# A selective scan followed by attention: output tiles of 32 times by four batches, one iteration behind the scan

## The reference, cut

```python
xr, gate = jnp.split(x @ W_in.T, 2, axis=-1)          # 1024 + 1024 channels
xn = layernorm(silu(conv4(xr + t_emb))) * ln_g + ln_b
Bm, Cm, dt = jnp.split(xn @ W_xproj.T, 3, axis=-1)    # 16 states each
def step(h, inputs):
    ad, bd, xt, ct = inputs
    h = jnp.clip(h * ad[:, :, None] + bd[:, :, None] * xt[:, None, :], -10.0, 10.0)
    yt = jnp.einsum('bd,bdh->bh', ct, h)
    return (h, yt)
_, ys = jax.lax.scan(step, h0, ...)                   # 1024 times
y = ys.transpose(1, 0, 2) + D * xn
x = x + y * silu(gate) @ W_out.T
...
x = x * s1[:, None, :]
x = (x - mu) * rsqrt(var + 1e-5)                      # per time, over 512
q, k, v = x @ q_weight, ...
```

## Time and profile before

| what | before |
|---|---|
| median of 3 runs | 2919.54 us (2915.05 to 2922.15) |
| the profiled execution's own time | 2919.2 us |
| its span | 2917.4 us |
| mean granted clock of PE | 0.965 |
| PE busy | 2700.9 us (93%) |
| DVE busy | 2012.0 us (69%) |
| POOL busy | 1258.6 us (43%) |
| ACT busy | 1191.2 us (41%) |
| bytes moved by transfers | 423.97 MB, 145 GB/s |

### The profile page before, as it was taken

The page is one execution under the profiler, slowest core; times in us unless marked ns, Lnnn a source line. Parts: engine busy times, 40 slices in busy tenths (PEclk is TensorE's granted clock), DMA queues, the critical chain, the costliest instruction groups (busy, mean ns, idle before and its releaser), DMA issues. The chain is left out here.

```text
span 2917.4 us, 54601 instructions
## 1 busy us (share of the span) xinstructions
PE 2700.9 (93%) x20561; PEld 1470.9 (50%) x20562; DVE 2012.0 (69%) x2121; ACT 1191.2 (41%) x2041; POOL 1258.6 (43%) x572
## 2 busy tenths in 40 slices
PE   7999955999999999999879999969999999999999
PEld 3444323666666666666558777833333333333337
DVE  2788866998888888888653333357777777777626
ACT  3677851211222211212231222126666666666641
POOL 0000001346555464555441221016667777777763
PEclk9999967999999999999889999979999999999999
DMA  3246474677777777777634334372334344354246
GB/s 105 93 159 208 177 249 99 144 165 165 170 164 170 167 169 162 173 162 168 177 124 155 136 148 169 130 201 68 81 88 124 92 123 115 88 127 119 83 170 228
DMA packets 255677, 423.97 MB, mean 145 GB/s; under 512 B 54760, under 2 KB 122984, under 8 KB 249144
## 3 DMA queue, kind: packets, MB, share of 16 engines
q1 hardware_dynamic: 172952, 332.71, 40.0%
q10 hardware_dynamic: 82592, 89.57, 13.0%
HBM read 260.91 MB, written 163.08 MB: 145 GB/s over the span
## 5 line engine op out<-in xcount | busy, mean ns | idle before, releaser
L909 DVE CUSTOM_DVE_ANT_0 b_h<-b_h,b_bx,b_bounds_all 128x512 f32<-128x512 f32 x1024 | 825.7, 806 | 148.8 <-PE b_bx L1043 98.8
L1609 DVE TENSOR_REDUCE e_half_max<-ef_banks 128x4 f32<-128x2048 f32 x256 | 586.3, 2294 | 235.1 <-PE ef_banks L1562 235.1
L1752 POOL TENSOR_TENSOR e_pair_sum<-e_probs 128x2048 f32<-128x2048 f32 x128 | 586.7, 4584 | 265.9 <-PE ef_banks L1601 214.4
L1721 ACT ACTIVATE e_probs<-ef_banks 128x512 f32<-128x512 f32 x1024 | 556.0, 595 | 311.5 <-PE ef_banks L1576 311.5
L1576 PE MATMUL ef_banks<-e_qs,e_ks 97*128 97x512 f32 x1024 | 383.1, 453 | 3.9 <-DVE e_half_max L1609 3.6
L1094 ACT COPY b_y_stage<-b_y_psum 128x128 f32<-128x128 f32 x256 | 68.6, 268 | 652.5 <-PE b_y_psum L1053 651.2
L1576 PEld LDWEIGHTS ef_banks<-e_qs,e_ks 97*128 97x128 f32 x1024 | 155.0, 189 | 332.1 <-ACT e_probs L1721 311.9
L1025 POOL TENSOR_TENSOR b_b_weights<-b_bd,b_mask_b 128x512 fp32r<-128x512 f32 x64 | 82.6, 1290 | 552.7 <-POOLq L836 459.2
L1043 PE MATMUL b_bx<-b_x_moving,b_b_weights 24*128 24x512 f32 x1024 | 256.3, 496 | 54.6 <-POOL b_c_weights L1027 27.4
L1053 PE MATMUL b_y_psum<-b_h,b_c_weights 128*32 128x128 f32 x8224 | 278.5, 276 | 0.5 <-ACT b_y_stage L1094 0.5
L1586 PE MATMUL ef_banks<-e_probs,e_v 128*32 128x512 f32 x2048 | 274.5, 608 | 0.5 <-ACT e_probs L1721 0.4
(11 more groups left out here) (225 smaller groups left out, 4076.4 us busy)
## 6 DMA issues: line engine op xcount, KB each, us to landing
b_x_moving<-xn_parts SPq DMA_DIRECT2D x252, 128.0 KB
e_ks<-qk_parts ACTq DMA_DIRECT2D x42, 512.0 KB, 4.8
e_qs<-qk_parts ACTq DMA_DIRECT2D x84, 256.0 KB, 3.5
xn_full<-a_xn SPq DMA_DIRECT2D x32, 512.0 KB, 3.2
xn_parts<-a_hi SPq DMA_DIRECT2D x64, 256.0 KB, 2.5
xn_parts<-a_lo SPq DMA_DIRECT2D x64, 256.0 KB, 2.5
silu_gate<-b_sg ACTq DMA_DIRECT2D x64, 256.0 KB, 7.1
scan_out<-b_y_stage ACTq DMA_DIRECT2D x256, 64.0 KB, 3.8
```

Source lines behind the costliest of these rows:

```text
L909: return nc.vector._custom_dve(bass.dve_ops.TENSOR_ADD_SAT, **operands)
L1609: nc.vector.tensor_reduce(out=half_max[:, u // UNITS % 2, :, r // NH, r % NH], in_=(banks[:, u % 2 * GROUP:(u % 2 + 1) * GROUP] if u < FIR ...
L1721: nc.scalar.activation(probs[:, g % 4, h, :], p_exp[h % 2], ACT.Exp).then_inc(exps, 1)
L1752: nc.gpsimd.tensor_tensor(out=pair_sum[:, t % 2], in0=probs[:, (2 * t) % 4], in1=probs[:, (2 * t + 1) % 4], op=ALU.add).then_inc(paired, 1)
```

## The change

Everything in it turns on the shape of an output tile. It now is 32 times of all four batches, so the tile of one scan iteration can be worked on one iteration later (`LAG` = 1).

- `load_mixed`, `load_y`, `load_x` and `load_x1` address DRAM as 4 batches × 32 times. xn and gate are loaded behind the second half's moving rows, no longer behind the first's.
- `load_moving` waits for `read` two pairs sooner; `load_bd` comes behind it and one half ahead.
- `take_turned` of half 0 of the next tile stands ahead of the iteration's last readout copy and its stores.
- W_out is loaded at the scan's start and split in iterations 0 and 1; the spread of B is issued in the block before. Output tiles start in iteration 1.
- The drain does the products of tile 30 and tile 31 in full. Seven x1 tiles are prepared there (five normalisations inside the projection's first steps); the eighth is loaded at its end and scaled (now by DVE), measured and normalised in steps 4 and 5 of batch 0. Batch 0's body is written out apart from the loop.
- `y_stage` and `sg` use the storage of `pj.v_rows`. In the last iteration two of four stores are issued by SP. The input array `x_tiles` is laid out in the new order of rows.

```diff
     def load_x1(self, sp, n, q):
-        sp.dma_start(self.x1[:, q, :], self.X1.rearrange("(q b) t c -> b q t c", b=BATCH)[bass.ds(n, 1)].rearrange("o q t c -> (o q) t c")[q]).then_inc(self.x_in[q], 16)
...
+        sp.dma_start(self.x1[:, q, :], self.X1.rearrange("(q i) (b t) c -> b q i t c", q=NQ, b=BATCH)[bass.ds(n, 1)].rearrange("o q i t c -> (o q) i t c")[q]).then_inc(self.x_in[q], 16)
...
 
-    LAG = P // STEPS
+    LAG = 1
     OUT_LAG = LAG + 1
...
-        y_stage = sb("y_stage", [128, 2, T // 4, 128], f32)
+        pj.late_rows()
+        y_stage, sg = (pj.v_rows[:, 2 * i:2 * i + 2, :] for i in range(2)); y_stage = y_stage.rearrange("p i (q c) -> p i q c", c=128)
...
+                spread_b(sp, Bx, spread, SEQ // PHASES * STATES, range(PHASES))
...
+        def load_mixed(sp, j):
             sp.wait_ge(gated, START + j)
-            sp.dma_start(xn, Xn[b, bass.ds(tq * P, P), :]).then_inc(xn_in, 16)
+            sp.dma_start(xn, Xn[:, bass.ds(j * STEPS, STEPS), :]).then_inc(xn_in, 16)
             for half in range(2):
                 sp.wait_ge(sg_out[half], START + j * 16 + 16)
             sp.dma_start(sg_in, SG[bass.ds(j, 1)].rearrange("o p c -> (o p) c")).then_inc(xn_in, 16)
-        def load_y(sp, j, tq, b, it):
+        def load_y(sp, j):
             for i in range(2):
-                sp.wait_ge(y_out[i], START + it * 64)
-            sp.dma_start(y[:], Y[bass.ds(tq * P, P)].rearrange("t (h b) c -> b t h c", h=2)[b]).then_inc(y_in, 16)
-        def load_x(sp, j, tq, b):
+                sp.wait_ge(y_out[i], START + j * 64 + 64)
+            sp.dma_start(y[:], Y[bass.ds(j * STEPS, STEPS)].rearrange("t (h b) c -> b t h c", h=2)).then_inc(y_in, 16)
+        def load_x(sp, j):
             sp.wait_ge(x1_ready, START + j)
-            sp.dma_start(x[:], I["x"][b, bass.ds(tq * P, P), :]).then_inc(res_in, 16)
+            sp.dma_start(x[:], I["x"][:, bass.ds(j * STEPS, STEPS), :]).then_inc(res_in, 16)
...
-        def sp_loop(sp, it, j, tq=None, b=None, store=False, before=None, more=True):
+        def sp_loop(sp, it, store=True, x=True, more=True, load_d=False):
+            j = it + (-1)
             for i in range(2):
-                sp.wait_ge(read, START + it * PAIRS + (10 + 8 * i))
-                load_bd(sp, it, i)
+                sp.wait_ge(read, START + it * PAIRS + (8 + 8 * i))
                 load_moving(sp, it, i)
                 if i == 0:
-                    if j is not None:
-                        load_mixed(sp, j, tq, b)
+                    sp.wait_ge(w_ready[1], START + it * 2 + (-1))
+                    load_bd(sp, it, 1)
+                elif more:
+                    sp.wait_ge(w_ready[0], START + it * 2 + 1)
+                    load_bd(sp, it + 1, 0)
             if more:
                 load_tile(sp, it + 1)
-            if j is not None:
-                load_y(sp, j, tq, b, it)
-                if store:
-                    store_x1(sp, j + (-2))
-                if before is not None:
-                    load_x(sp, j + (-1), *before)
...
+            if load_d:
+                sp.wait_ge(out_split, START + 4)
+                sp.dma_start(d_row, I["D"].rearrange("(o n) -> o n", o=1).to_broadcast([P, INNER])).then_inc(d_in, 16)
+            load_mixed(sp, j)
+            load_y(sp, j)
+            if store:
+                store_x1(sp, j + (-2))
+            if x:
+                load_x(sp, j + (-1))
+
+
+        def pool_loop(pool, it, j, out=False, split=True, low=False, split_out=False):
             for i in range(2):
                 if i == 1 and split:
                     split_low(pool, it)
+                if i == 1 and split_out:
+                    for c in range(4):
...
-        def act_loop(act, it, j, more=True, split_out=False):
+        def send_y(e, it, i, parts):
+            dst = Y[bass.ds(it * STEPS + i * T, T)].rearrange("(q s) r (j c) -> j (s r) q c", s=4, j=4)
+            for part in parts:
+                e.dma_start(dst[part], y_stage[32 * part:32 * part + 32, i]).then_inc(y_out[i], 16)
+
+        def act_loop(act, it, j, more=True, split_out=False, ahead=None):
             for q in range(STEPS // 4):
                 i = (4 * q) // T
-                if q == 0 and j is not None:
-                    take_turned(act, j, 0)
                 if q == 1 and j is not None:
                     take_turned(act, j, 1)
                 if q == 7 and j is not None:
                     take_out(act, j)
+                if q == 7 and ahead is not None:
+                    take_turned(act, ahead, 0)
                 act.wait_ge(read, START + it * PAIRS + (BEFORE + 2 * q + 4))
                 if (4 * q) % T == 0:
                     act.wait_ge(y_out[i], START + it * 64)
                 nc.scalar.copy(y_stage[:, i, q % (T // 4), :], y_psum[:, 0:128]).then_inc(y_free, 1)
                 if (4 * q + 4) % T == 0:
                     act.wait_ge(y_free, START + it * (STEPS // 4) + (q + 2))
-                    dst = Y[bass.ds(it * STEPS + i * T, T)].rearrange("(q s) r (j c) -> j (s r) q c", s=4, j=4)
-                    for part in range(4):
-                        act.dma_start(dst[part], y_stage[32 * part:32 * part + 32, i]).then_inc(y_out[i], 16)
+                    send_y(act, it, i, range(4) if more or i == 0 else range(2))
 
                 if q == 0:
                     take_gate(act, it, 0)
...
             def _(sp):
+                sp.dma_start(w_out_plain, I["w_out_t"].rearrange("(m p) n -> p m n", p=P)).then_inc(out_in, 16)
                 load_tile(sp, 1)
-                spread_b(sp, Bx, spread, SEQ // PHASES * STATES, range(PHASES))
...
-                sp.dma_start(w_out_plain, I["w_out_t"].rearrange("(m p) n -> p m n", p=P)).then_inc(out_in, 16)
...
+                sp.wait_ge(w_ready[0], START + 1)
+                load_bd(sp, 1, 0)
+                sp_loop(sp, 1, False, False, load_d=True)
+                sp_loop(sp, 2, False)
+                with sp.Fori(3, LOOPS - 1) as it:
+                    sp_loop(sp, it)
+                sp_loop(sp, LOOPS - 1, more=False)
+                sp.wait_ge(y_free, START + LOOPS * (STEPS // 4) + 1)
+                send_y(sp, LOOPS - 1, 1, range(2, 4))
...
+                pool_loop(pool, 1, 0, split_out=True)
+                pool_loop(pool, 2, 1, low=True)
...
+                load_mixed(sp, last)
+                sp.wait_ge(x1_out, START + (last - 3) * 16)
+                for q in early_tiles[:3]:
+                    pj.load_x1(sp, 0, q)
+                load_y(sp, last)
+                store_x1(sp, last - 2)
+                load_x(sp, last - 1)
+                for q in early_tiles[3:]:
+                    pj.load_x1(sp, 0, q)
+                sp.dma_start(pj.w_u[:], I["u_t"].rearrange("(k p) n -> p k n", p=P)).then_inc(pj.u_in, 16)
+                store_x1(sp, last - 1)
+                load_x(sp, last)
+                for i in range(2):
+                    sp.wait_ge(sg_out[i], START + LOOPS * 16)
+                    sp.wait_ge(y_out[i], START + LOOPS * 64)
                 pj.spread_rows(sp)
-                store_x1(sp, last - 1)
-                load_x(sp, last, NQ - 1, BATCH - 1)
                 store_x1(sp, last)
+                sp.wait_ge(x1_out, START + TILES * 16)
+                pj.load_x1(sp, 0, NQ - 1)
...
+                for g in range(2):
+                    take_turned(act, last - 1, g)
+                pj.split_high(act, 0)
+                take_out(act, last - 1)
+                for g in range(2):
+                    take_turned(act, last, g)
+                for n in (1, 2):
+                    pj.split_high(act, n)
+                pj.root(act, 0, slice(0, NQ - 1))
+                for q in range(2):
                     pj.normalise(act, 0, q)
                 take_out(act, last)
...
+                add_x(dve, nc.vector, last - 2)
+                mix(dve, nc.vector, last)
+                pj.split_low(dve, 0)
+                pj.stats_of(dve, 0, early_tiles[:3])
+                add_x(dve, nc.vector, last - 1)
+                pj.split_low(dve, 1)
+                pj.split_low(dve, 2)
+                pj.stats_of(dve, 0, early_tiles[3:])
+                pj.add_eps(dve, 0, slice(0, NQ - 1))
+                pj.invert_std(dve, 0, slice(0, NQ - 1))
                 add_x(dve, nc.vector, last)
...
-            with e.Fori(0, BATCH - 1) as b:
+            body(0, True, True)
+            with e.Fori(1, BATCH - 1) as b:
                 body(b, True)
             body(BATCH - 1, False)
...
                                 nc.vector.tensor_tensor(out=lo[:, e % 2, :], in0=p_qk[e % 2][:], in1=hi[:, e % 2, :].bitcast(f32), op=ALU.subtract).then_inc(lo_ready, 1)
+                        if first and s == 4:
+                            pj.scale_x1(dve, nc.vector, 0, NQ - 1, True)
+                            pj.stats_of(dve, 0, (NQ - 1,))
+                            pj.add_eps(dve, 0, slice(NQ - 1, NQ))
+                        if first and s == 5:
```

(4 more changed lines are left out.)

192 lines of the change are left out of this document (65 added, 127 removed).

## The result

The changed kernel takes 3119.12 us (median of four runs, 3109.13 to 3122.01) against 2920.02: 1.068 times as long, 95% interval 1.065 to 1.071. The forecast was 2938, with a range that ended at 3010. The profiled execution's span is 3120.0 us, PE's mean clock 0.929.

The account below looks back on a forecast made before the run. The scan was taken as DVE's chain, with PE busy 28.8 us per iteration and able to catch up little. Scan +44.5, ahead of it 0, drain -26 and projection +0.5 gave +19 on 2919.2: 2938 us, range 2858 to 3010.

Parts of the forecast that it names:

- Which engines the loads run on: Scan: the loads of xn, y and x, with 4 in front of their sources, run on 4 of 16 engines.
- How long an iteration gets: Scan: 31.5 us per iteration, bounds 29.0 and 33.5; from iteration 1's start 974.5 against 930.0 us, +44.5.
- the sum over one of the four engines: Scan, from an iteration's start S: transfer times on one engine added up; y lands at S + 21.7, moving rows S + 28.8.
- 24 GB/s per engine for y, x and the moving rows behind them: Scan loads: rate taken from the spread of B; xn and y 5.5 us each, x 2.7.
- y's place: SP's second burst in the scan: y directly behind xn and gate, with 1.5 us put in for ACT's stores.
- The idle quarter: DMA engines in the scan: about a quarter idle between bursts, which slower transfers can use up before costing anything.
- A queue behind the queue: Rival, chance 0.15: in the scan late y delays mix, turn, stores and next y; 34.5 us an iteration, 3025 us.
- All 16 engines: Rival, chance 0.11: SBUF's 128 partitions spread the scan's loads; 29.0 us an iteration, drain -39, 2852 us.
- Enough idle time: Rival, chance 0.22: same four engines, late transfers fall into the scan's idle quarter; 29.8 us an iteration, 2888 us.
- Ahead of the scan: Before iteration 1: the earlier spread of B and the w_out load together change 0 us, between -11 and +8.
- The drain: Scan's end to the projection's first transpose: two output tiles left instead of five, 77.2 to 51 us; -26, between -39 and -20.
- The turned tile ahead of the copy: Scan: with earlier moving rows returns at most 1.3 us per iteration of PE's waits; 29.0 us at best.

Follow-up runs that it names:

- turn_after_stores: The changed kernel with the first take_turned back at the next iteration's head, behind the readout copy and the stores: 3120.0 us against 3119.1.
- time_major: The changed kernel with output tile rows ordered time, batch, so that the sources of xn, y and x begin with 32: 2833.6 us, 2835.5 when repeated.

## Why the prediction was wrong

**Which engines the loads run on: right.** 3.8 of 16 engines were busy in xn's window, and a loss of this size appears and disappears with the first dimension of the source. The Trainium skill (DMA: Bandwidth & Descriptors, "Why a DMA increments its semaphore by 16 and not by 1") has the rule of the prediction, the largest number up to 16 that divides the slowest dimensions of both sides, and the trace agrees with it: 4 in front, 3.8 engines. The same section of the Trainium skill says that a transfer takes the lowest-numbered engines, so that the eight-row transfers of moving rows would share the four. The trace has no engine's number, but its packets fit: 32 of the 96 rows came late. That is 4 engines with one row each of all eight transfers; if the eight-row transfers lay elsewhere, it would be 16.

**How long an iteration gets: wrong, 31.5 us against 37.4.** Scan +44.5 forecast, +219.4 measured; this is nearly the whole error. The step that failed is the sum over one of the four engines, above all its rate, and with it the overlap that was to hide what was late. The short iterations have the forecast length, 31.6 us, but not by the sum's terms: xn is issued up to 6.4 us before S, where the sum had it run from S + 7.3, so that agreement is partly luck. The long ones, 43.1 us, the sum did not foresee.

1. *24 GB/s per engine for y, x and the moving rows behind them.* I took the rate of the spread, which ran alone. xn does run at 26 once the moving rows are through. But y and x overlap the next moving rows, and then the mean of the 16 engines was 9.2 GB/s. The packets' own times in the trace say the same of the loads: on SP's queue a packet of 2 KB took 93 ns on average from 1122 to 1124, and 370 ns from 1126 to 1128. This is no effect of the narrow loads. In the kernel before, with moving rows beside xn on 16 engines, stands

```profile
1006.00:1008.00 2.00, 2.00 (x20) 1.29 (x12) 1.89 (x4) 0.27 (x1) 0.40 (x1) 1.00 0.97 141
```

which is 9.1 GB/s per engine. A milder warning stood in a row that I used for something else: 181 GB/s at 0.76 in the earlier trace rows is 14.9. So y took 13.6 us from issue to use in the iteration shown (1120.58 to 1134.16, POOL's row, not shown) where the sum had 7.5, and the moving rows 22.0 us from issue to PE's release where it had 12.3: S + 39.0 in place of S + 28.8, and S + 43.8 in the usual long one. Even x alone, 2.7 us in the sum, cost 117 us in all.

2. *y's place.* The sum let y start right behind the gate, at S + 14.2, and counted 1.5 us for ACT's stores, not that y waits for them. In the iteration shown this did no harm: y was issued at S + 14.1. In the usual long one it was issued at S + 17.3, and the next moving rows behind it at S + 20.1 in place of S + 16.5. That the stores land late because a quarter of each stands behind xn is my reading; no run isolates it.
3. *The idle quarter.* I let it absorb what was late. It is a mean of 16 engines. xn at 1114 and the rest of y and x at 1134 do run in it, but on some 4 engines while the others have little or nothing to do, and a third of the next moving rows needs just these four.

On top of these comes PE's clock, which the sum left out. In the earlier trace rows PE has 1.00 over the scan; here it is 0.90, since every long iteration has a stretch at 0.50 at its stall, and PE's busy time per iteration grew from 28.8 to 32 × 476.18 / 514 = 29.6 us.

**The rivals.** "A queue behind the queue", to which I gave 0.15, named the right thing, late loads that make later ones late, and held ACT's wait for the turn to be a link. turn_after_stores shows that this link is real but small, 1.7 us an iteration, and paid back by what PE gains. Its 34.5 us an iteration was too low as well. "All 16 engines" gave 2852; with xn, y and x on 16 engines the kernel takes 2834 to 2867. For "Enough idle time" I let the sum turn negative below 30.4 us an iteration; by its own terms that is 31.5 - 19 / 29 = 30.8.

**Ahead of the scan:** 0 forecast, +3.4 measured. **The drain:** -26 forecast, -19.0 measured, outside its bound of -20. The sum had y at +24, the last addition at +46 and the first transpose at +51 behind the scan's end; they came at +27.4, +49.1 and +58.2. The addition waited for ACT's copy (2.05 us) and not for x. SP's issue, 5.50, 4.88 and 10.61 us, was not in the sum; how much of the delay is its doing is not shown. With xn, y and x on 16 engines it is -38.5, the bound of -39. **The projection:** +0.5 forecast, -1.2 measured: the moved work is hidden. **The turned tile ahead of the copy:** with the moving rows I allowed 1.3 us an iteration and took PE's 28.8 us of busy time as a floor, "29.0 at best". Alone it returns 35 us in the kernel before and 41 in time_major, and time_major's iteration takes 28.4 us with PE busy throughout: the 28.8 still held time that could go.

## What to carry to other kernels

Before a tile's rows are regrouped, look at what the first dimension of each transfer's source becomes: here 4 in front of 32 in place of 128 cost 252 to 285 us, and with 32 in front of 4 the kernel is faster than before. Take an engine's rate from rows in which it does what it will do then, with the same neighbours; GB/s divided by 16 and by the busy share gives the mean. A transfer that uses few engines is as long as their queues, and everything that later uses these engines stands behind it, an idle share of the whole notwithstanding.

## What the runs showed of the hardware that was not expected

- The DMA engines' rate falls while moving rows run: 26 GB/s for each engine with xn nearly alone (0.20 MB in 2 us at 23.9%), 9.2 on average with y, x and moving rows together (0.42 MB in 3 us at 95.3%), and 9.1 in the kernel before (141 GB/s at 0.97). Which resource they share was not tried.
- Issues on SP's queue take long behind narrow transfers that are still under way: 0.35 to 0.6 us for a load as a rule, 25.76 us for the x tile behind the spread from sources of 4 and 2, 0.58 us for the same load behind the spread from sources of 16, 10.61 us for four x1 loads in the changed kernel's drain. The x tile load isn't narrow itself.
- A stall for a transfer cost PE twice here: it ran at the lower clock after it, 0.50 in the window 1145.4 to 1149 behind 9.8 us of waiting. In the drain, behind 17.4 us, its four transposes took 1.09 us where they took 0.63 in the kernel before.
